# Decoder layer on one core: the experts' weight loads stand between the attention's last stores

## What is computed

```python
x = x + attn(layernorm(x))   # 16 heads, 8 keys per query at a stride of 8, ternary weights, its own residual
x = x + xattn(layernorm(x), ctx)  # 64 context rows a batch; scores below the 54th largest are dropped
x = x + ffn(layernorm(x))    # a shared expert, and the best 4 of 16 routed experts
# ffn, routed part
scores = sigmoid(gate_w @ x) + gate_b
weights, indices = top_k(scores, 4); weights = weights / weights.sum(-1)
routed = sum over the 4 of: weight * (silu((x @ w1[e]) * (x @ w3[e])) @ w2[e])
```

## Time and profile before

| | us |
|---|---|
| median of 3 runs | 757.45 |
| the runs | 754.23, 757.45, 760.1 |
| profiled execution | 759.45 |
| its span, first to last instruction | 757.6 |
| mean granted clock of TensorE | 0.928 of full speed |

### The profile page before, as it was taken

The page is one execution under the profiler, slowest core; times in us unless marked ns, Lnnn a source line. Parts: engine busy times, 40 slices in busy tenths (PEclk is TensorE's granted clock), DMA queues, the critical chain, the costliest instruction groups (busy, mean ns, idle before and its releaser), DMA issues. The chain is left out here.

```text
span 757.6 us, 15757 instructions
## 1 busy us (share of the span) xinstructions
PE 628.3 (83%) x4034; PEld 541.6 (71%) x4034; DVE 578.3 (76%) x1750; ACT 414.8 (55%) x1134; POOL 456.0 (60%) x360
## 2 busy tenths in 40 slices
PE   1888869978689999989575119999999999999994
PEld 1776758857555676566352118999999999999993
DVE  5899957999876887747637528888888888888883
ACT  4886535531246655454341217767666666666662
POOL 3557493536204444466766633777777776878875
PEclk9999898999799999999787659999999999999998
DMA  9920000300166565633336334788888887888885
GB/s 291 306 66 29 24 19 29 112 29 16 55 237 208 176 204 207 232 130 130 109 131 231 137 103 91 124 138 141 142 143 142 143 140 116 147 148 147 144 125 57
DMA packets 76950, 100.32 MB, mean 132 GB/s; under 512 B 9728, under 2 KB 70160, under 8 KB 76304
## 3 DMA queue, kind: packets, MB, share of 16 engines
q0 software_dynamic: 26736, 37.64, 27.5%
q1 hardware_dynamic: 47952, 59.58, 26.3%
q10 hardware_dynamic: 2176, 2.10, 0.9%
HBM read 50.91 MB, written 52.95 MB: 137 GB/s over the span
## 5 line engine op out<-in xcount | busy, mean ns | idle before, releaser
L1627 POOL DMA_INDIRECT out_dram<-yw,xg x143 | 222.0, 1552 | 87.8 <-issue 59.7
L1133 POOL DMA_INDIRECT xs_scratch<-rows,slot x128 | 126.0, 985 | 123.4 <-DMA xs_scratch<-rows,slot 81.4
L336 POOL TENSOR_TENSOR pv<-v_sb,pr 128x256 f32<-128x256 f32 (+7 forms) x32 | 68.5, 2153 | 66.0 <-DVE pr L325 47.6
L1510 PE MATMUL cbank<-w_hi,xtc_hi 128*128 x286 | 105.6, 369 | 1.6 <-DVE xtc_lo L1522 0.9
L1510 PE MATMUL cbank<-w_hi,xtc_lo 128*128 x286 | 93.4, 327 | 0.0
L1510 PE MATMUL cbank<-w,xtc_hi 128*128 x286 | 92.6, 324 | 0.0
L1510 PE MATMUL cbank<-w_hi,stc_hi 112*128 (+1 forms) x286 | 81.2, 284 | 1.0 <-DVE stc_hi L1592 1.0
L1499 PE MATMUL cbank<-identb,xg 128*128 128x128 f32 x286 | 55.6, 276 | 31.5 <-DMA xg<-xs_scratch 31.5
L1510 PE MATMUL cbank<-w_lo,stc_hi 112*128 (+1 forms) x286 | 81.0, 283 | 0.0
L1564 DVE TENSOR_TENSOR hh<-cbank,h 128x176 f32<-128x176 f32 x143 | 48.8, 341 | 41.7 <-ACT h L1558 41.4
L1570 ACT ACTIVATE sgc<-hh 128x128 f32<-128x128 f32 x143 | 44.4, 311 | 60.5 <-DVE hh L1564 60.1
(11 more groups left out here) (230 smaller groups left out, 1632.5 us busy)
## 6 DMA issues: line engine op xcount, KB each, us to landing
xg<-xs_scratch SPq DMA_DIRECT2D x143, 144.0 KB, 2.7
w<-w13r_dram SPq DMA_DIRECT2D x8, 704.0 KB, 6.7
w_hi<-ctx_t_dram SPq DMA_DIRECT2D x8, 512.0 KB, 4.6
w_hi<-x_scratch SPq DMA_DIRECT2D x8, 512.0 KB, 4.3
out_dram<-w_hi SPq DMA_DIRECT2D x16, 256.0 KB, 2.7
w_lo<-w2r_dram SPq DMA_DIRECT2D x4, 1024.0 KB, 9.2
xs_scratch<-pads_dram SPq DMA_DIRECT2D x1, 2304.0 KB, 11.2
xs_scratch<-pad_row SPq DMA_DIRECT2D x16, 144.0 KB, 1.8
```

The costliest lines, as they stand in the source:

```text
L336: f_pv.sig(nc.gpsimd.tensor_tensor(pv[:, m % PVR, 0:w, :].rearrange("p l (h d) -> p l h d", h=H), v_sb[:, a, at:at + w, :].rearrange("p l ...
L1133: nc.gpsimd.indirect_dma_start(t["xs"], bass.IndirectOffsetOnAxis(ap=slot[:, n % 2, k:k + 1].bitcast(U32), axis=0), rows[:, n % NROW, k // ...
L1510: last = nc.tensor.matmul(out, stationary, moving, start=j == 0, stop=j == len(pairs) - 1)
L1627: nc.gpsimd.indirect_dma_start(t["out"], bass.IndirectOffsetOnAxis(ap=xg[:, p, ID:ID + 1].bitcast(U32), axis=0), yw[:, p % YB, :], None, c ...
```

## The change

The 12 pieces are no longer loaded in the turns. SP loads them between the stores of pairs 10 to 15, each piece as soon as what lay in its place has been used: w2 after the last reading of keys and products (`keys_read`), w13 by and by after the stores of the pairs that lay there (`rows_stored` now takes a range), after the last reading of the values (`values_read`) and after the last add (`added`). The attention's buffers lie in another order: k_sb and prod now come before pv, so that w2_lo (32768 bytes of a partition) covers k_sb and the first 10240 bytes of prod, and xh comes before ot. `rows` moves behind `rdenb` and lies over pv and later buffers. So xhC of group 0 waits for `weighed_read`, and `zeros` is in two steps: `prt` at the old place, `rows` and `hsr` behind add:15 (`zeros:1`). In VectorE's order stA:3 moves from ahead of choose:0 to behind spread:0. ctx_t 2 is loaded after store 10 instead of 13, ctx_t 3 after store 11, x1 3 after store 13 instead of 14. The number of DMAs and of computing instructions stays the same. In the diff, the extended tuples of names are left out.

```diff
@@ -91,12 +91,12 @@
     wv_t = sb("wv_t", [P, DC, D], R32)
     xt_hi, xt_lo = (sb(n, [P, 2, 2, DC, P], R32) for n in ("xt_hi", "xt_lo"))
     x_of.append(sb("x_second", [P, WIN, 2, D]))
-    v_sb, ot, xh = sb("v_sb", [P, 2, KR, D]), sb("ot", [P, 2, 2, DC, P]), sb("xh", [P, 2, D])
+    v_sb, xh, ot = sb("v_sb", [P, 2, KR, D]), sb("xh", [P, 2, D]), sb("ot", [P, 2, 2, DC, P])
+    k_sb, prod = sb("k_sb", [P, 2, KR, D]), sb("prod", [P, 2, WIN, H, DH + 1])
     pv, wo_t = sb("pv", [P, PVR, WIN, D]), sb("wo_t", [P, DC, D])
     xt_f, pr, sc = sb("xt_f", [P, 2, DC, P]), sb("pr", [P, 2, 2, WIN, H]), sb("sc", [P, 2, WIN, H])
     qk_scale, vo_scale = sb("qk_scale", [P, 1]), sb("vo_scale", [P, 1])
     mv, ve, rs = sb("mv", [P, 2 * PAIRS, 2]), sb("a_ve", [P, 2, 2 * PAIRS]), sb("a_rs", [P, 2, 2 * PAIRS])
-    k_sb, prod = sb("k_sb", [P, 2, KR, D]), sb("prod", [P, 2, WIN, H, DH + 1])
     nm, rs1, rq = (sb(n, [P, 2 * PAIRS]) for n in ("nm", "rs1", "rq"))
     g_col, power = sb("g_col", [P, DC]), sb("power", [P, 2, 2 * QUAD])
     stats, mx = sb("stats", [P, 2, 2, 6]), sb("mx", [P, 2, H])
...
@@ -442,10 +442,18 @@
         for k in range(WIN):
             eng.wait_ge(s_st[k], 16)
 
-    def rows_stored(eng):
-
-        for j in range(WIN, PAIRS):
+    def rows_stored(eng, first=WIN, last=PAIRS - 1):
+
+        for j in range(first, last + 1):
             eng.wait_ge(s_st[j], 16)
+
+    def values_read(eng):
+
+        f_pv.wait(eng, PAIRS - 1)
+
+    def weighed_read(eng):
+
+        f_o.wait(eng, PAIRS - 1)
 
     def keys_read(eng):
...
@@ -709,7 +717,6 @@
     xh2 = late[:, 0:G].rearrange("p (t d) -> p t d", t=GT)
     x2 = late[:, G:(1 + NX2) * G].rearrange("p (g t d) -> p g t d", g=NX2, t=GT)
     xt3 = late[:, (1 + NX2) * G:(1 + NX2 + NX3) * G].rearrange("p (g c n) -> p g c n", g=NX3, c=DC)
-    rows = sb("rows", [P, NROW, GT, ROW])
     mx = sb("mxb", [P, GT])
     neg = sb("neg", [P, GT, NCTX])
     neg2 = sb("neg2", [P, GT, NCTX])
...
@@ -720,6 +727,7 @@
     prt = sb("prt", [P, GT, P])
     den = sb("denb", [P, GT])
     rden = sb("rdenb", [P, GT])
+    rows = sb("rows", [P, NROW, GT, ROW])
     th = sb("th", [P, GTOK])
     sg = sb("sg", [P, GT, NE])
     t8 = sb("t8", [P, GT, 8])
...
@@ -802,6 +810,8 @@
             att.first_rows_stored(eng)
 
     def row_free(eng, n):
+        if n == 0:
+            att.weighed_read(eng)
         if n >= NROW:
             rows_landed(eng, n - NROW)
...
@@ -1211,16 +1221,15 @@
             at = eng.value_load(keep["pad_at"][0:1, e:e + 1], min_val=e * SLOTS, max_val=(e + 1) * SLOTS - P)
             eng.dma_start(t["xs"][bass.ds(at, P), :], pre.pad_row[:, :]).then_inc(s_pads, 16)
 
-    def load_weights(eng, k):
-
-        s_w = keep["s_w"]
-        if k < 2 * DC * 2:
-            ch, e = k % DC, slice(k // DC * NE // 4, (k // DC + 1) * NE // 4)
-            eng.dma_start(keep["w13"][:, ch, e, :], t["w13r"][ch, :, e, :]).then_inc(s_w, 16)
-        else:
-            c, half = (k - 4 * DC) % 2, (k - 4 * DC) // 2
-            e = slice(half * NE // 2, (half + 1) * NE // 2)
-            eng.dma_start(keep["w2_lo"][:, c, e, :].bitcast(F32), t["w2r"][c, :, e, :]).then_inc(s_w, 16)
+    def load_w13(eng, ch, quarter):
+
+        e = slice(quarter * NE // 4, (quarter + 1) * NE // 4)
+        eng.dma_start(keep["w13"][:, ch, e, :], t["w13r"][ch, :, e, :]).then_inc(keep["s_w"], 16)
+
+    def load_w2(eng, c, half):
+
+        e = slice(half * NE // 2, (half + 1) * NE // 2)
+        eng.dma_start(keep["w2_lo"][:, c, e, :].bitcast(F32), t["w2r"][c, :, e, :]).then_inc(keep["s_w"], 16)
 
     def table(eng, n):
...
@@ -1279,11 +1288,13 @@
 
     def zeros(eng, n):
 
-        att.first_rows_stored(eng)
-        nc.vector.memset(rows[:, :, :, ID:ROW], 0.0).then_inc(s_zero, 1)
-        nc.vector.memset(prt[:, :, :], 0.0).then_inc(s_zero, 1)
-        nc.vector.memset(hsr[:, :, :], 0.0).then_inc(s_zero, 1)
-        eng.wait_ge(s_zero, 3)
+        if n == 0:
+            nc.vector.memset(prt[:, :, :], 0.0).then_inc(s_zero, 1)
+        else:
+            att.added(eng)
+            nc.vector.memset(rows[:, :, :, ID:ROW], 0.0).then_inc(s_zero, 1)
+            nc.vector.memset(hsr[:, :, :], 0.0).then_inc(s_zero, 1)
+        eng.wait_ge(s_zero, 1 + 2 * n)
 
     def sync_turn(eng, i):
...
@@ -1295,12 +1306,8 @@
             store_out(0)(eng, i - 3)
         if 3 < i + 2 < NG:
             load_ct(eng, i + 2)
-        if i < PIECES // 2:
-            load_weights(eng, 2 * i)
         if 0 <= i - 3:
             store_out(1)(eng, i - 3)
-        if i < PIECES // 2:
-            load_weights(eng, 2 * i + 1)
 
     def finish(eng):
...
@@ -1368,8 +1375,8 @@
         """
         passage["v"] = """
             stA:0 add:9 root:0 scores:14 add:10 weigh:13 scores:15 weigh:14 zeros:0 negs:0 add:11 tops:0 weigh:15 masks:0
-            stA:1 add:12 root:1 x2_:0 add:13 stC:0 stA:2 add:14 root:2 negs:1 tops:1 masks:1 add:15 stA:3 choose:0
-            shares:0 spread:0 x2_:1 stC:1 negs:2 root:3 tops:2 masks:2 hsr_:0 x2_:2 hs_:0 stC:2 stA:4 choose:1 root:4
+            stA:1 add:12 root:1 x2_:0 add:13 stC:0 stA:2 add:14 root:2 negs:1 tops:1 masks:1 add:15 zeros:1 choose:0
+            shares:0 spread:0 stA:3 x2_:1 stC:1 negs:2 root:3 tops:2 masks:2 hsr_:0 x2_:2 hs_:0 stC:2 stA:4 choose:1 root:4
             shares:1 spread:1 hsr_:1 xf_0:0 xf_1:0 negs:3 tops:3 masks:3 stA:5 hs_:1 choose:2 shares:2 x2_:3 stC:3 hsr_:2
             root:5 spread:2 xf_0:1 xf_1:1 negs:4 tops:4 masks:4 stA:6 x2_:4 stC:4 root:6
         """
...
@@ -1395,14 +1402,32 @@
             att.first_rows_stored(eng)
             for n in range(NX1):
                 pre.load_x1(eng, t, n)
-            for j in range(WIN + 1, PAIRS):
+            for j in range(WIN + 1, WIN + 3):
                 att.store(eng, j)
-                if j == PAIRS - 3:
-                    cross.load_ct(eng, 2)
-                if j == PAIRS - 2:
-                    cross.load_x1(eng, NX1)
-                    cross.load_ct(eng, 3)
-            att.rows_stored(eng)
+            cross.load_ct(eng, 2)
+            att.keys_read(eng)
+            for half in range(2):
+                for c in range(2):
+                    cross.load_w2(eng, c, half)
+            att.store(eng, WIN + 3)
+            att.rows_stored(eng, WIN, WIN + 2)
+            cross.load_w13(eng, 0, 0)
+            cross.load_ct(eng, 3)
+            att.store(eng, WIN + 4)
+            att.values_read(eng)
+            for piece in range(3):
+                cross.load_w13(eng, 1, piece)
+            att.store(eng, WIN + 5)
+            cross.load_x1(eng, NX1)
+            cross.load_w13(eng, 0, 3)
+            att.store(eng, WIN + 6)
+            att.rows_stored(eng, WIN + 3, WIN + 5)
+            cross.load_w13(eng, 0, 1)
+            att.store(eng, WIN + 7)
+            att.rows_stored(eng, WIN + 6)
+            att.added(eng)
+            cross.load_w13(eng, 0, 2)
+            cross.load_w13(eng, 1, 3)
             cross.table_load(eng)
             for i in range(NG + LAST):
                 cross.sync_turn(eng, i)
```

More of the change, by code:

```diff
@@ L79, in wait @@
             eng.wait_ge(self.sem, v)
-AttentionPart = namedtuple("AttentionPart", "run store start ops first_rows_stored rows_stored keys_read products_read "
-                           "queries_read sums_read turned_read added")
+AttentionPart = namedtuple("AttentionPart", "run store start ops first_rows_stored rows_stored values_read weighed_read keys_read "
+                           "products_read queries_read sums_read turned_read added")
 def attention_part(nc, t, cross, banks, sb, sem, flow):
@@ L554, in attention_part @@
              weigh=weigh, values=values),
-        first_rows_stored, rows_stored, keys_read, products_read, queries_read, sums_read, turned_read, added)
+        first_rows_stored, rows_stored, values_read, weighed_read, keys_read, products_read, queries_read, sums_read, turned_read, added)
 class TileTable:
@@ L689, in load @@
         eng.dma_start(t["out"][TOK + P:N_OUT, :], t["pads"][P:P + N_PAD, 0:D]).then_inc(self.s_pad, 16)
-CrossPart = namedtuple("CrossPart", "run ops sync_turn finish load_x1 load_ct table_load")
+CrossPart = namedtuple("CrossPart", "run ops sync_turn finish load_x1 load_ct load_w13 load_w2 table_load")
 def cross_part(nc, t, keep, R, sb, sem, flow, att):
@@ L1316, in cross_part @@
                hs_=hs_, g1_=g1_, xf_0=xf_0, xf_1=xf_1, ys_0=ys_0, ys_1=ys_1)
-    return CrossPart(run, ops, sync_turn, finish, load_x1, load_ct, table_load)
+    return CrossPart(run, ops, sync_turn, finish, load_x1, load_ct, load_w13, load_w2, table_load)
 def front_phase(nc, t, keep, outer):
```

## The result

The changed kernel takes 752.09 us (median of 11 runs, 749.85 to 753.87). The kernel before, run beside it, has a median of 757.45 over 11 runs. The ratio is 0.9926, with a 95% interval from 0.9902 to 0.995: 5.4 us less. The two intervals overlap from 0.9902 to 0.9918, which is 6.2 to 7.4 us less. The profiled executions give 751.15 (span 749.4) against 759.45 (span 757.6): the span is 8.2 us shorter. The forecast was 10.0 less.

What follows compares the result with a forecast made beforehand. It took POOL's chain of 128 scatters, two in flight, as the bound. Weights out of the turns gave -10.8 and stA:3's move +0.8, so -10.0: 747.4 us from the 757.45 median, range 739 to 758.

Steps and rivals of the forecast that it cites:

- B: Rival, hardly a gain: remaining turn traffic costs x1's price per KB, or slots become the bound; 2.8 off, 754.6; chance 0.22.
- Step 1: Turns beside the scatters: taking the 12 weight loads out saves 10.8 us, readings ranging from 3.6 to 18.0.
- Step 2: Loads issued between 177 and 219 us, where DMA has room; queue clear when the scatters begin, so no cost.
- Step 3: Waiters on SP's queue: x1 3 lands near 210, its reader stA:3 comes at 226; all free.
- Steps 4, 5 and 7: Splitting zeros, xhC:0's wait for weighed_read and the buffers' new order: each costs or gains nothing.
- Step 6: VectorE: stA:3 behind spread:0 makes group 1's slots 1.4 us later, its first scatter 0.8 later.
- What is late next: Scatters stay slower than the slots (22.8 us a group); the 4.03 wait shrinks, and the expert phase is unchanged.
- A: Rival, larger gain: out and ctx_t alone hardly disturb the scatters, 0.5 a turn; 17 off, 740; chance 0.2.
- C: Rival, slower: loads crowd x1 3 in SP's ring, delaying stA:3 and group 1's slots; 761.4 if landing at 240; chance 0.08.

Runs made afterwards that it cites:

- second comparison: The changed kernel measured again, with one register operation added to GpSimd's wait in the expert phase, against the kernel before: 750.89 us, ratio 0.9882.
- a2: The changed kernel with only the 12 weight loads put back into the turns; buffer order, zeros and VectorE order stay: 759.92 us, ratio 1.0005.
- a1: The changed kernel again, with one register operation added to GpSimd's wait in the expert phase: 750.89 us, ratio 0.9882 to the kernel before.
- a4: The changed kernel, loading only one column in 64 of ctx_t for groups 4 to 7 (output differs): 743.05 us, ratio 0.9776.
- c1: The changed kernel, with the output stores of groups 0 to 3 writing 2 rows of 128 (output differs): 747.16 us, ratio 0.9865.
- b1: The changed kernel with four scatters in flight instead of two (FLY = 4), no pause between them: 829.23 us, ratio 1.0784.
- c2: The changed kernel with four scatters in flight and a GpSimd memset with a wait for its end between scatters: 743.4 us, ratio 0.9826.
- b3: The changed kernel with three scatters in flight instead of two: 810.97 us, beside 769.02 of the kernel before; no ratio given.

## Why the prediction was right, and which term was off

**What bounds the kernel: right.** The scatter chain's end and the end of the program keep 315.1 us between them in every kernel whose scatters don't hold up the other engines.

**The total: near, in part by luck.** From the median the forecast was 747.4, and the first comparison's 752.09 lies 0.1 outside the 743 to 752 that the forecast gave itself, nearer to B's 754.6. The second comparison's 8.8 less is nearer to the forecast's 10.0. The mechanism is shown by a2.

**Step 1, the weights out of the turns: right in kind, too large.** I took 10.8 saved, the middle of 9.0 (a straight line through two prices) and 12.5 (shares by bytes); the trace has 7.7 in the three turns. The mis-sized term is what stays in a turn: I had it at 8.7 us for the three (19.5 less 10.8), 2.9 each, and it measured 4.0, 3.8 and 4.0 (a1: 4.2, 5.2 and 4.1, which leaves 6.0 saved). Of my readings the straight line (3.5 a turn, 9.0 saved) was the nearest to the changed kernel's trace; the value I took was 3.1 too high, x1's own price (5.3 a turn, 3.6 saved) 4.1 too low. In the changed kernel's trace the loads of x1 gave 1.6 that I hadn't counted, so the stretch gained 9.3 where I had 10.8. In a1 they gave 0.3, and the stretch gained 6.8: that the first trace came so near was in part luck. Whether a rule by bytes can hold at all stays open after a4 and c1.

The prediction weighed this against a rule. Turns of 3072 KB cost 6.5 and 7.0 us, turns of 1024 KB 3.8 to 4.0 (5.2 once in a1). The Trainium skill (DMA: Bandwidth & Descriptors, Queues, rings and completion order) has each DMA engine serve the rings it has work for in turn, packet by packet. Three times the bytes cost less than twice the loss, as the prediction expected of such turn-taking, but the loss isn't flat, so turn-taking alone doesn't give it. The prediction put the strict form of that rule at the 3.6 of rival B without a working, and 7.7 (a1: 6.0) was saved.

**Step 2, the loads' new place: right.** Predicted issues 177, 184, 197.6, 204.5, 208.7, 218.6; measured 176.0, 183.0, 197.0, 203.9, 208.2, 217.6. DMA share over 177 to 227 went from 0.33 to 0.68, and the first scatter came at 226.63 (226.95 before).

**Step 3, who waits for SP's queue: right.** stA:3 has no wait before it.

**Steps 4, 5 and 7, zeros, xhC and the layout: right.** VectorE's idle time ahead of choose:0 is 3.90 us now and was 3.04, and a2 has all three edits, with stA:3 behind spread:0, and stands at 1.0005.

**Step 6, stA:3 behind spread:0: right.** 1.4 on group 1's slots was forecast, 31.92 less 30.60 is 1.3, and it is 1.2 to 1.9 over the other runs. The 17th scatter was forecast at 258.95, 0.8 later than before; it came at 258.38, 0.2 later.

**What is late next: nothing was.** 1.1 us of the gain went again behind the 49th scatter. No slot waits for a scatter any more (4.03 us at 328.94 before), and group 7's were written at 390.51. The last scatter came at 434.33 for 432.6 forecast.

**The rivals.** A (the rest of a turn disturbs little, 740) fell with the 4.0 a turn. B (x1's price per KB, 754.6) was much nearer by its price, 5.3 a turn, than A's 0.5, but its second half, slots that take 26.4 us a group, isn't in the trace: from 257.39 to 390.51 six groups take 22.2 each. C (x1 3 late) is excluded by stA:3's row.

## What to carry to other kernels

A chain that waits for its own DMAs pays for every transfer that others put into the machine beside it. Find where such a chain runs, and move bulk loads to a stretch in which nobody waits for a landing; but price what stays behind by an experiment that shrinks it, for the three prices worked out from bytes lay between 3.6 and 12.5 us. Look next at the depth of the chain: with twice the DMAs in flight and a short pause between their issues, waits for landings went from 69.0 to 4.3 us, and that edit alone, on the kernel before, gave as much as the change did.

## What the runs showed of the hardware that was not expected

Indirect DMAs issued by GpSimd every 1.26 us without a wait (b1, sixteen in a row) went with waits of 3.5 to 7.0 us on VectorE and ScalarE beside group 0's scatters and of up to 13.95 us beside later ones, on TensorE too, ended by "remote"; SP's load of ctx_t 4 was issued at 249.65 instead of 234.6. At 1.46 us a step with the same four lanes (c2) none of them appears. The whole kernel is 829 us (beside 769 of the kernel before) with the one and 743 (beside 756) with the other. What holds the other engines' semaphores back isn't shown, nor where between 1.26 and 1.46 us the limit lies, nor whether it is the memset and its wait themselves or only the time they take. Three lanes (b3) fell into it as well: its profiled run of 814.14 has 17 rows with such waits from 220 to 430 us, up to 13.1 us long.
